# Macaron block, one core: VectorE's side work and a one-chunk start in the experts, tile numbers and low weights on GpSimd in the routing

## The reference

```python
x = x + 0.5 * ffn(layernorm(x), Wg, W_in, W_out)
x = x + attention(layernorm(x), Wq, bq, Wk, bk, Wv, bv, Wo, bo, J_attn, lambda_attn)
x = x + 0.5 * ffn(layernorm(x), Wg, W_in, W_out)
```

## Time and profile before

| | |
|---|---|
| median of 3 runs | 1773.65 us (1771.53 to 1775.53) |
| the profiled execution | 1788.82 us |
| its span | 1787.0 us |
| granted TensorE clock, mean | 0.903 of full speed |
| TensorE, VectorE, ScalarE, GpSimd busy | 83%, 61%, 39%, 34% of the span |

### The profile page before, as it was taken

The page is one execution under the profiler, slowest core; times in us unless marked ns, Lnnn a source line. Parts: engine busy times, 40 slices in busy tenths (PEclk is TensorE's granted clock), DMA queues, the critical chain, the costliest instruction groups (busy, mean ns, idle before and its releaser), DMA issues. The chain is left out here.

```text
span 1787.0 us, 26109 instructions
## 1 busy us (share of the span) xinstructions
PE 1487.0 (83%) x8708; PEld 1103.7 (62%) x8708; DVE 1097.2 (61%) x2666; ACT 692.9 (39%) x1064; POOL 615.8 (34%) x540
## 2 busy tenths in 40 slices
PE   6279999999547566999999999996582799999995
PEld 2268888888536454555555555542442688888884
DVE  7745555555277576887777777770357455555551
ACT  3123333333123220466665666664031233333331
POOL 1045555653314246111111111111300456555533
PEclk9589999999868885899999999997795899999997
DMA  8234444452367999164553644601470344444425
GB/s 285 71 91 95 95 95 95 93 97 30 70 195 223 279 286 248 52 167 110 132 154 95 161 124 120 170 18 38 161 239 8 92 96 95 95 95 95 95 30 124
DMA packets 145185, 219.63 MB, mean 123 GB/s; under 512 B 19584, under 2 KB 107648, under 8 KB 141952
## 3 DMA queue, kind: packets, MB, share of 16 engines
q1 hardware_dynamic: 108464, 167.14, 32.1%
q0 software_dynamic: 30720, 42.62, 15.1%
q10 hardware_dynamic: 5904, 8.66, 1.7%
HBM read 128.20 MB, written 94.11 MB: 124 GB/s over the span
## 5 line engine op out<-in xcount | busy, mean ns | idle before, releaser
L602 POOL DMA_INDIRECT sums<-e_res,e_sum_row x160 | 253.3, 1583 | 307.9 <-ACT e_res L717 282.3
L1353 ACT ACTIVATE a_wts<-a_s_psum 128x1024 f32<-128x1024 f32 (+1 forms) x384 | 294.7, 809 | 145.3 <-PE a_s_psum L1418 143.7
L1304 DVE CUSTOM_DVE_ANT_0 a_masked<-a_m_psum,mask 128x128 bf16<-128x128 f32 (+3 forms) x512 | 240.1, 487 | 111.2 <-PE a_m_psum L1395 101.1
L1395 PE MATMUL a_m_psum<-a_kp,a_qp 96*128 96x512 f32 (+2 forms) x768 | 279.5, 409 | 20.0 <-PEq L906 12.7
L1395 PEld LDWEIGHTS a_m_psum<-a_kp,a_qp 96*128 96x128 f32 x768 | 149.6, 197 | 141.1 <-DVE a_parts L1307 50.7
L226 POOL DMA_INDIRECT e_slots<-normalized,e_token x160 | 163.9, 1025 | 202.3 <-DVE e_token L415 148.8
L1283 POOL TENSOR_SCALAR_AFFINE_SELECT a_wts<-a_wts 128x512 f32<-128x512 f32 x128 | 78.1, 634 | 443.6 <-ACT a_wts L1353 443.6
L1418 PE MATMUL a_s_psum<-a_qp,a_kp 97*128 97x512 f32 (+2 forms) x768 | 211.1, 358 | 2.4 <-ACT a_wts L1353 2.2
L707 ACT ACTIVATE e_act_a<-e_a_psum 128x512 f32<-128x512 f32 (+1 forms) x192 | 100.8, 527 | 286.4 <-PE e_a_psum L779 237.5
L645 DVE TENSOR_TENSOR e_hid<-e_act_a,e_g_psum 128x512 f32<-128x512 f32 (+1 forms) x192 | 114.6, 597 | 155.8 <-PE e_g_psum L779 132.0
L794 PE MATMUL e_o_psum<-e_w_hi,e_h_hi 128*128 128x256 f32 x640 | 182.8, 286 | 0.0
(11 more groups left out here) (201 smaller groups left out, 2519.8 us busy)
## 6 DMA issues: line engine op xcount, KB each, us to landing
packs<-q_pack SPq DMA_DIRECT2D x64, 512.0 KB, 5.9
e_w_raw<-in_W_in SPq DMA_DIRECT2D x16, 1024.0 KB, 8.2
a_qp<-packs SPq DMA_DIRECT2D x16, 1024.0 KB, 7.7
a_kp<-packs SPq DMA_DIRECT2D x16, 1024.0 KB, 14.4
e_w_raw<-in_W_out SPq DMA_DIRECT2D x16, 512.0 KB, 7.9
normalized<-r_xn SPq DMA_DIRECT2D x16, 512.0 KB, 4.3
sums<-x_res SPq DMA_DIRECT2D x2, 4096.0 KB, 17.8
values<-q_vals SPq DMA_DIRECT2D x32, 256.0 KB, 4.2
```

Source lines behind the costliest of these rows:

```text
L602: nc.gpsimd.indirect_dma_start(sum_dram, bass.IndirectOffsetOnAxis(ap=sum_row[:, at:at + 1], axis=0), res[j][:], None, bounds_check=last_r ...
L1304: nc.vector.tensor_tensor_reduce(masked[at][:, 0:width], seen, c["mask"][:, QC - width:], 1.0, MASKED, ALU.add, ALU.max, top).then_inc(max ...
L1353: nc.scalar.activation(wts[(u * NS + s) % 2][:, j, 0:w], s_ps[q % 2][:, 0:w], ACT.Exp).then_inc(weighed, 1)
L1395: nc.tensor.matmul(m_ps[bank((n, h, z))][:, 0:stream], qp[n % NB][0:PACK, h, qt * P:(qt + 1) * P], kp[n % NB][0:PACK, h, part * QC:part * ...
```

## The change

It has four parts.

1. Routing, low weights: VectorE's one subtraction (L362) goes. GpSimd makes three of 128x1024, each after ScalarE's cast of that part (`w_split`).
2. Routing, numbers: the tile numbers of the first BY_POOL = 3 pieces are made by GpSimd after `is_column` of that piece (`is_made`) and, for the third, after TensorE's reading of the first; VectorE makes only the last piece's. TensorE waits for a new semaphore, `numbers_made`, and VectorE waits for it before it writes `is_column` of a third or fourth piece.
3. Experts: the first pair of experts is written out before the loop, which has two turns left. In the first expert only chunk 0 is transposed ahead of the products; chunk 1 is transposed after block f = 1, chunk 2 after block f = 3, and the high and low parts follow in the same places. In every expert VectorE's gates come after the first block of hidden(1), the first low weights after its second block; before, both stood ahead of hidden(1).
4. Projections: the statistics of batch 1 come after half 0 of batch 0, those of batches 2 and 3 after half 1.

```diff
--- before.py
+++ after.py
@@ -247,6 +247,7 @@
     U = NT // CH
     PIECES = 4
     N = NK // PIECES
+    BY_POOL = 3
     HALVES = [slice(0, U), slice(U, NT)] if r == 0 else [slice(0, NT)]
     with ExitStack() as ctx:
         sb = lambda n, s, dt=F32: kit.sb(f"r{r}_{n}", s, dt, ctx)
...
@@ -309,6 +310,17 @@
                 nc.gpsimd.memset(gates[:], 0.0).then_inc(gates_clear, 1)
                 link(nc.gpsimd.iota(number_i[:], pattern=[[1, NK]], base=1, channel_multiplier=0))
                 nc.gpsimd.tensor_copy(number[:], number_i[:]).then_inc(numbered, 1)
+                for z, (a, b) in enumerate(W_PARTS):
+                    pool.wait_ge(w_split, z + 1)
+                    nc.gpsimd.tensor_tensor(held["lo"][0][:, a:b], held["raw"][:, a:b], held["hi"][0][:, a:b].bitcast(F32), ALU.subtract).then_inc(w_rest, 1)
+                pool.wait_ge(numbered, 1)
+                for z in range(BY_POOL):
+                    kts = slice(z * N, (z + 1) * N)
+                    pool.wait_ge(is_made, z + 1)
+                    if z >= 2:
+                        pool.wait_ge(piece_read, z - 1)
+                    nc.gpsimd.tensor_tensor(valued[z % 2][:, :, SLOTS:], is_column[z % 2][:],
+                                            number[:, kts].unsqueeze(2).to_broadcast([P, N, SLOTS]), ALU.mult).then_inc(numbers_made, 1)
                 pool.wait_ge(rows_out, 16 * (NT // 4))
                 pool.wait_ge(gates_out, 16)
                 pool.wait_ge(list_ready, 1)
@@ -358,9 +370,6 @@
                     nc.vector.tensor_copy(hot_bf[:, :, tiles, :], hot[:, :, tiles, :]).then_inc(hot_ready, 1)
 
                 choose(0)
-                dve.wait_ge(w_split, len(W_PARTS))
-                nc.vector.tensor_tensor(held["lo"][0][:], held["raw"][:], held["hi"][0][:].bitcast(F32),
-                                        ALU.subtract).then_inc(w_rest, 1)
                 choose(1)
 
                 flat = lambda a: a[:].rearrange("p k t -> p (k t)")
@@ -387,14 +396,16 @@
                     kts = slice(z * N, (z + 1) * N)
                     if z >= 2:
                         dve.wait_ge(lane_made, z - 1)
+                        dve.wait_ge(numbers_made, min(z - 1, BY_POOL))
                         dve.wait_ge(piece_read, z - 1)
                     nc.vector.tensor_tensor(is_column[z % 2][:], c["spots"][:, 0:SLOTS].unsqueeze(1).to_broadcast([P, N, SLOTS]),
                                             flat(column)[:, kts].unsqueeze(2).to_broadcast([P, N, SLOTS]), ALU.is_equal).then_inc(is_made, 1)
                     nc.vector.tensor_tensor(is_within[z % 2][:], c["spots"][:].unsqueeze(1).to_broadcast([P, N, P]),
                                             flat(within)[:, kts].unsqueeze(2).to_broadcast([P, N, P]), ALU.is_equal).then_inc(within_made, 1)
-                    dve.wait_ge(is_made, z + 1)
-                    nc.vector.tensor_tensor(valued[z % 2][:, :, SLOTS:], is_column[z % 2][:],
-                                            number[:, kts].unsqueeze(2).to_broadcast([P, N, SLOTS]), ALU.mult).then_inc(column_made, 1)
+                    if z >= BY_POOL:
+                        dve.wait_ge(is_made, z + 1)
+                        nc.vector.tensor_tensor(valued[z % 2][:, :, SLOTS:], is_column[z % 2][:],
+                                                number[:, kts].unsqueeze(2).to_broadcast([P, N, SLOTS]), ALU.mult).then_inc(column_made, 1)
                     if z == 0:
                         link(nc.vector.tensor_tensor(best[:], best[:], keep[:], ALU.mult))
                         link(nc.vector.tensor_tensor(sums[:], best[:, 0, :], best[:, 1, :], ALU.add))
@@ -523,7 +534,10 @@
                 for kt in range(NK):
                     if kt % N == 0:
                         pe.wait_ge(within_made, kt // N + 1)
-                        pe.wait_ge(column_made, kt // N + 1)
+                        if kt // N < BY_POOL:
+                            pe.wait_ge(numbers_made, kt // N + 1)
+                        else:
+                            pe.wait_ge(column_made, kt // N + 1 - BY_POOL)
                         pe.wait_ge(lane_made, kt // N + 1)
                     last = nc.tensor.matmul(listed_ps, is_within[kt // N % 2][:, kt % N, :], valued[kt // N % 2][:, kt % N, :], start=(kt == 0), stop=(kt == NK - 1))
                     if kt % N == N - 1:
@@ -570,7 +584,9 @@
 
         def in_turn(eng, body):
 
-            with eng.Fori(0, EXP // 2 - 1) as i:
+            body(0, 0, True, True)
+            body(0, 1, True)
+            with eng.Fori(1, EXP // 2 - 1) as i:
                 body(i, 0, True)
                 body(i, 1, True)
             body(EXP // 2 - 1, 0, True)
@@ -627,10 +643,10 @@
                     nc.vector.tensor_tensor(s_lo[:, :, c0:c0 + n], tp[:, :, 0:n],
                                             s_hi[:, :, c0:c0 + n].bitcast(F32), ALU.subtract).then_inc(s_lo_done, 1)
 
-                def body(i, u, more):
+                def body(i, u, more, first=False):
                     e = i * 2 + u
 
-                    def hidden(ci):
+                    def hidden(ci, between={}):
                         n = CHUNKS[ci][1]
                         h = (u * NC + ci) % 2
 
@@ -649,10 +665,12 @@
                             dve.wait_ge(h_hi_done, m + 1)
                             nc.vector.tensor_tensor(h_lo[h][:, f, 0:n], hid[q][:, 0:n],
                                                     h_hi[h][:, f, 0:n].bitcast(F32), ALU.subtract).then_inc(h_lo_done, 1)
-
-                    def gates(e, u, tile):
+                            if f in between:
+                                between[f]()
+
+                    def gates():
                         for ci, (c0, n) in enumerate(CHUNKS):
-                            dve.wait_ge(slots_in[u][ci], (tile + 1) * 16 * (n // P))
+                            dve.wait_ge(slots_in[u][ci], (i + 1) * 16 * (n // P))
                         for k in range(TOPK):
                             nc.vector.tensor_tensor(by_choice[k][:], slots[u][:].rearrange("p (j w) -> p j w", w=ROW)[:, :, D + k],
                                                     held["choice"][k][:, bass.ds(e * ST, ST)], ALU.mult).then_inc(gate_parts, 1)
@@ -666,12 +684,15 @@
                         nc.vector.tensor_tensor(w_lo[1 - u][:, a:b], w_raw[:, a:b], w_hi[1 - u][:, a:b].bitcast(F32),
                                                 ALU.subtract).then_inc(w_rest, 1)
 
-                    hidden(0)
-                    slots_lo(e, 2)
-                    gates(e, u, i)
+                    if first:
+                        hidden(0, {1: lambda: slots_lo(e, 1), 3: lambda: slots_lo(e, 2)})
+                    else:
+                        hidden(0)
+                        slots_lo(e, 2)
+                    between = {0: gates}
                     if more:
-                        weights_rest(0)
-                    hidden(1)
+                        between[1] = lambda: weights_rest(0)
+                    hidden(1, between)
                     if more:
                         weights_rest(1)
                         weights_rest(2)
@@ -681,7 +702,6 @@
                         slots_lo(e + 1, 1)
 
                 slots_lo(0, 0)
-                slots_lo(0, 1)
                 in_turn(nc.vector, body)
 
             @block.scalar
@@ -760,10 +784,10 @@
                             last = nc.tensor.transpose(tp[:, k, j * P:(j + 1) * P], slots[u][:, at:at + P], c["ident"][:])
                     last.then_inc(s_tposed, 1)
 
-                def body(i, u, more):
+                def body(i, u, more, first=False):
                     e = i * 2 + u
 
-                    def up(ci):
+                    def up(ci, between={}):
                         c0, n = CHUNKS[ci]
                         pe.wait_ge(s_lo_done, e * NC + ci + 2)
                         if ci == 0:
@@ -780,6 +804,8 @@
                                                             s[:, k, c0:c0 + n], start=(z == 0),
                                                             stop=(z == len(terms) - 1))
                                 last.then_inc(done, 1)
+                            if f in between:
+                                transposes(e, u, i, between[f])
 
                     def down(ci):
                         c0, n = CHUNKS[ci]
@@ -797,8 +823,11 @@
                             last.then_inc(o_done, 1)
 
                     next_tile = i + u
-                    up(0)
-                    transposes(e, u, i, 2)
+                    if first:
+                        up(0, {1: 1, 3: 2})
+                    else:
+                        up(0)
+                        transposes(e, u, i, 2)
                     up(1)
                     down(0)
                     up(2)
@@ -810,7 +839,6 @@
                     down(2)
 
                 transposes(0, 0, 0, 0)
-                transposes(0, 0, 0, 1)
                 in_turn(nc.tensor, body)
 
 
@@ -903,6 +931,7 @@
```

(5 more changed lines are left out.)

22 lines of the change are left out of this document (13 added, 9 removed).

## The result

The changed kernel takes 1778.15 us in the median of 20 runs (1771.9 to 1785.15), the kernel before 1774.12 us in the median of 20 (1769.54 to 1778.14). The ratio is 1.0025, 95% interval 1.0014 to 1.0037: slower by 4.4 us (2.5 to 6.6), where 2.7 us slower were forecast. The forecast lay inside the 0.2% that it called no change; its chances were 0.38 for faster, 0.36 for slower and 0.26 for neither, so the sign was no more than an even choice.

A forecast was written before the change was run, and what follows sets the result against it. VectorE was taken to pace the routing, where TensorE idles, and the projections. Routing +10.6, start -9.5, order 0 and statistics +1.6 gave +2.7 us on 1773.65: 1776.4 us, own range 1771 to 1782, whole range 1757 to 1786.

The forecast's parts named there:

- low weights: Routing's choice: GpSimd's three subtractions hold VectorE's steps with two SBUF operands, +1.7 us per routing.
- numbers: Routing's pieces: GpSimd's tile numbers and VectorE's L391 and L393 take turns, +3.6 us per routing.
- start, both stages: Start of the experts: first product after chunk 0 alone, -5.5 and -4.0 us, together -9.5 us.
- order: Experts, chunk 1: gates and low weights behind the first and second hidden value gain 0; upper gain 11.7 us.
- statistics: Projections: splitting the statistics costs VectorE 2.7 us, small waits take up about 1.1; +1.6 us, between 0 and +3.
- My doubt at this step: Start of the experts: TensorE's results are seen late while GpSimd issues gathers; 1.0 us allowed, all in the second start.
- the row at 168.31: Second expert: VectorE took a gate block ended at 165.18 only at 168.31; read as side work not holding it.
- the 1.1 us of small waits: Projections: VectorE's small waits in the next halves were to take up about 1.1 us of the statistics' +2.7.
- nothing is held: Rival, routing: VectorE and GpSimd run beside each other, routing -10.5 us, time 1755.3 us; chance 0.15.
- short steps first: Rival, routing: the choice's short steps pass between GpSimd's subtractions, L391 and L393 cannot; 1770.9 us; chance 0.15.
- the order removes the waits: Rival, experts: VectorE's queue made the waits, so some 8 of 11.7 us go; 1765.4 us; chance 0.15.
- The early start gains nothing: Rival, experts' start: results seen late until the last gather, chunk 1 starts where it did; 1785.9 us; chance 0.12.

The follow-up runs named there:

- E1: The kernel before with no edit, run again for a second trace; 1775.61 us, ratio 1.0002.
- E2: The kernel before with only the low weights moved to GpSimd; 1777.31 us, ratio 1.001 against before.
- E3: The kernel before with only the tile numbers of three pieces moved to GpSimd; 1779.29 us, ratio 1.0018 against before.
- E11: The changed kernel run again beside the kernel before; 1777.35 us against 1773.72, ratio 1.0008.
- E7: The kernel before with only VectorE's order in chunk 1 changed; 1791.82 us against 1793.59, ratio 0.9997.
- E5: E3's edit plus VectorE's row of counts copied to PSUM and read there, against the kernel before; 1783.72 us against 1793.59, ratio 0.9949.
- E6: The kernel before with only the experts' start on one chunk, VectorE's order unchanged; 1789.45 us against 1793.59, ratio 0.9974.

## Why the prediction was right, and where it was not

The mean was near and the sign right, and the mechanism that carried it is shown. But three of the terms were off: the routing by -3.3 us, the start by +2.7, the statistics by +1.5. That they cancel to +0.9 is luck. Per routing unless said; E1 is the trace of before:

| step | forecast | measured |
|---|---|---|
| low weights | +1.7 | +1.45 (changed, E2) |
| numbers | +3.6 | +2.2 (changed, E3) |
| start, both stages | -9.5 | -7.5 (changed), -6.1 (E11), to the second expert |
| order | 0 | 0 within 0.3% (E7) |
| statistics | +1.6 | +3.1 in the mean (2 to 4) |
| sum | +2.7 | 2 x 3.65 - 6.8 + 3.1 = +3.6; by the times +4.4 |

**Low weights.** As argued, step for step: L364, L365 and L367 were held, each to the end of one subtraction. The second half began 12.43 us after the first instead of 10.98.

**Numbers.** Right that VectorE is held, wrong in the size: I had put 2.7 us of GpSimd for each piece, by the line through 512 and 1024 float32 elements. The instruction takes 2.33 us alone (E5) and keeps VectorE for 2.1 to 2.2. The operands are bf16; the line was drawn through rows of another type, and gave 2.83. A piece became 5.74 us and not 6.3. The 0.3 us that were taken off for the last piece did not come: three times 0.73 us are the whole 2.2.

**Start.** The first product came 4.30 us after the first transposes, as worked out (97.5 - 93.2). The gain after it was over-sized for two reasons. The base was a trace with late signals, in which chunk 1 started 31.6 us after the first gather; in E1 it is 30.0 (115.60 - 85.61). And in the first stage TensorE runs longer at its lower level: in the changed kernel the products reach the higher one at 108.41, 5.3 us after the first, with ahead of them one group of transposes and a wait of 2.36 us; in E1 they reach it at 105.7, 3.0 us after, with two groups ahead of them. So it is in the mean too, but not each time: 2.7 us (1.3 to 4.4) in 16 stages with the old start, 4.6 (2.9 to 6.2) in 12 with the new one; in the second stage it was 3.2 in the changed kernel and 4.4 in E1. That the fewer transposes ahead are the cause is not shown. Granted clock by stretch, changed kernel and then E1:

```profile
92.00:104.00 12.00, 2.81 (x10) 0.50 0.54 171
104.00:109.00 5.00, 5.00 (x14) 0.55 0.72 207
109.00:114.00 5.00, 5.00 (x27) 1.00 0.39 108
```
```profile
92.00:104.00 12.00, 4.91 (x19) 0.50 0.64 211
104.00:109.00 5.00, 5.00 (x20) 0.84 0.40 108
```

(The columns are the stretch, its length, TensorE's busy us and instructions, the granted clock, the DMA share and GB/s.) The start begins the work sooner by 5 us, and 2.0 us of these go to products at the lower level and to the eight transposes that now stand among them, in the first stage.

**Late signals.** My doubt at this step named the right thing and priced it wrongly, as 1.0 us in all. It is nothing on one occasion and, by one trace, the whole gain on another (E6). It also spoilt the reading of the order: I used the row at 168.31 as evidence that the order is worth nothing, and that row was a late signal. The conclusion held by luck, for a simpler reason: without late signals there is next to nothing to gain (3.3 us of waits, none over 0.2).

**Statistics.** The cost on VectorE was right in the first part (5.5) and 8.7 instead of 8.2 in the second. What failed is the 1.1 us of small waits that were to take part of it up: nothing was taken up.

Of the rivals, *nothing is held* and *short steps first* are out by the rows above, *the order removes the waits* by E1 and E7. *The early start gains nothing* is out where signals are in time, and E6's trace shows it where they are late.

## What to carry to other kernels

Work moved from VectorE to an idle GpSimd was free here only where VectorE's instructions beside it read no more than one operand from SBUF. So move one of VectorE's operands to PSUM first (here a change from +2.2 to -3.7 us per routing, the copy counted, with the same split of the work), or put the work into a gap of VectorE's own. Before a stage's waits are priced from one profile, take a second profile of the same kernel: 8.4 us of waits in this one were of the occasion, not of the kernel.
